# A state-space scan on one core: sums of h\*C in four 64x64 tiles of TensorE, and dt\*u\*B of every state by whole 128x128 products

## The chip, the cores and the metric

The kernel runs on one core of a Trainium2 chip. A core has TensorE (matrix products into PSUM, 8 banks of 512 fp32 per partition), VectorE, ScalarE and GpSimd (elementwise work), and SyncE, whose queue issues DMA transfers here. The engines run their own instruction streams and meet at semaphores. The metric is the device time of one execution in microseconds (us), lower is better, as a median of several runs.

## The reference

A decoder of two layers on 8 sequences of 128 tokens with 256 features, all in fp32. The change lies in the second layer's first part, a state-space (Mamba) block with 512 inner channels and 16 states per channel:

```
xz = einsum('bld,ed->ble', rmsnorm(x) * norm_w, in_proj_w);  x_inner, z = split(xz)
xc = silu(causal_conv4(x_inner) + conv_b)
x_ssm = einsum('bld,ed->ble', xc, x_proj_w)            # 16 B, 16 C, 1 dt per token
dt = softplus(x_ssm[..., -1:] * dt_w + dt_b);  A = -exp(A_log)
for each token t:                                       # per channel and state
    h = exp(dt_t * A) * h + (dt_t * u_t) * B_t          # u = xc
    y_t = sum over states (h * C_t) + D_param * u_t
out = einsum(y * silu(z), out_proj_w) + residual
```

Ahead of it lie two attentions and a mixture of experts, behind it a WKV recurrence and a ternary feed-forward part. The change does not touch those.

## The kernel before

Channels lie on partitions (4 channel tiles, `CT`, of 128), the 1024 tokens along the free axis. The scan loop has `SLOTS` = 64 slots, one for each channel tile and state. Slot s belongs to state `state(s)` and channel tile `channels(s)`: the first 32 slots take channel tiles 0 and 1 in turn through the 16 states, the last 32 take tiles 2 and 3. The hand-written streams do for each slot:

- ScalarE, `decay(s)` (L1694): dA = exp(dt \* A) into one of four buffers.
- TensorE, `dBu_in(s)` (L1523): makes dt\*u\*B in PSUM, in one of two pairs of banks (4, 5 and 6, 7). States 0, 4, 8, 12 are `DIRECT`: B's row is spread over the partitions by a bf16 product with a selector (L1529; B was split by GpSimd into three bf16 parts, `split`), and VectorE multiplies it by dt\*u in place (`dBu_of`, L1824). The other states are "turned": dt\*u was once transposed to tokens on partitions (`turn_dtu`, L1520; ScalarE's copy `turned_dtu`, L1682), ScalarE scales it by B per token (`scaled`, L1709, eight instructions of 128x256 for the two slots of a state), and eight transposes (L1536) turn it back.
- VectorE, `scan(s)` (L1834): one `tensor_tensor_scan` of 128x1024 gives h.
- GpSimd (L1911): hC = h \* C, where C's row was spread over the partitions by a DMA (SyncE, L1440).
- TensorE, `y_sum(s)` (L1548): adds hC to y in PSUM banks 0 to 3, by two products with the identity (L1557), one for each half of the tokens, 128 rows and 512 columns. For a channel tile's first state `skip_term` (L1546) adds D\*u in the same way.

TensorE's order in the loop is written out: at step s first `dBu_in(s + 1)`, which waits until scan s-1 has freed the banks, then `y_sum(s - 2)`. At the end two of the four channel tiles are projected out early (L1586 to L1590, rows at L1424), then come the last two y sums, and VectorE's gates (L1841). An fp32 product shows in the trace as two MATMUL records (two passes), a transpose as one.

Before the loop: GpSimd gathers the experts' rows (L1873), VectorE adds them up (`combine`) and takes the norm (L1332 to L1334). ScalarE writes the selector (`sel`, L1597), takes magnitudes of the last part's weights, makes the ternary weights (L1341 to L1344), and then the root that L1332 waits for. TensorE does the input projections (L1446), six of the eight tiles of z behind the rest of the prelude, B, C and dt rows (L1460), and dt's spread (L1467). VectorE and ScalarE make dt (`steps`, `exponentials`, L1677, `dt_and_dtu`, L1773 and L1775).

Two other places of the kernel, in the attentions and the expert part, use parts of the TensorE array: `values` (L676) writes two products of 64 output rows each to the partitions 0 to 63 and 64 to 127, between whole products of lines L658, L648, L667 and L686, and the bias products of L1472 have 32 rows each:

```python
for e in range(2):     # L675, in values(i)
    t = eng.matmul(ps[e * R:(e + 1) * R, 5, 0:2 * P], layer[name]["kvn"][:, b, :], prT[:, i % 2, :, e, :],
                   start=True, stop=True)
...
for b in range(NB):    # L1470
    rows = slice((b % 4) * E, (b % 4 + 1) * E)
    t = eng.matmul(ps[:, b, 0:D], weightT[rows, b // 4], bias_dn[rows],
                   start=True, stop=True)
```

Of the whole ones, `queries` (L648, with 96 rows) and `scores` (L658) are four products each in eight records, `turn_probs` (L667) is four transposes in four, and `output` (L686) two products in four.

## Time and profile before

| | us |
|---|---|
| median of 3 runs | 880.86 (879.38 to 882.98) |
| the profiled execution | 879.86 |
| its span | 877.7 |
| TensorE busy | 722.6 (82%) |
| VectorE busy | 695.3 (79%) |
| ScalarE busy | 550.1 (63%) |
| GpSimd busy | 515.2 (59%) |

The span is that of the instructions, and the rest of the profiled execution's time lies around it. Times in the rows are microseconds from the span's start, unless a row gives mean ns. PE is TensorE's products, PEld its weight loads, DVE VectorE, ACT ScalarE, POOL GpSimd, and L1834 is line 1834 of the kernel. The ends of TensorE's records are modelled and overlap the next record, so its pace is read from starts. The busy shares are means over stages with different limits. They do not say what a slot of the scan costs.

### The profile page before, as it was taken

The page shows a single profiled execution, that of the slowest core. Times are in us where ns is not written, and L with a number is a line of the kernel's source. Part 1 is how long each engine was busy: PE and PEld are TensorE (multiplying, and loading weights), DVE is VectorE, ACT ScalarE, POOL GpSimd, SP SyncE. Part 2 cuts the span into 40 slices and gives each one's busy share as a digit, 9 for nine tenths or more (in the row PEclk, how much of TensorE's full clock was granted, in tenths as well). Part 3 has the DMA queues.
Part 4 walks back from the last instruction along what each step waited for, and adds up shares of the span by engine and source line. Part 5 has one row for each costly group of instructions (what it writes and reads, how often), then busy time and mean ns, then how long its engine had stood idle before and what let it go on. Part 6 is the DMA issues. An engine that isn't in the chain of part 4 may idle for free. (4 is left out here: it accounts for less than half of the span.)

```text
span 877.7 us, 14518 instructions
## 1 busy us (share of the span) xinstructions
PE 722.6 (82%) x4318; PEld 530.6 (60%) x4321; DVE 695.3 (79%) x1515; ACT 550.1 (63%) x1383; POOL 515.2 (59%) x545
## 2 busy tenths in 40 slices
PE   5899999999999886299999149869899999961465
PEld 3588888888888774198897024345455555641333
DVE  6777788888898874877787456796999999769957
ACT  2545555555565553276676766688998788209286
POOL 2067777777777863255553572437999899624211
PEclk9999999999999999599999559979999999995679
DMA  8735000000000500058857330032322223010001
GB/s 318 240 145 240 1 1 1 8 1 7 8 1 7 206 7 13 19 165 214 237 164 124 90 102 19 3 119 70 99 97 96 87 92 110 0 49 0 0 13 36
DMA packets 30171, 70.52 MB, mean 80 GB/s; under 512 B 5456, under 2 KB 19472, under 8 KB 28176
## 3 DMA queue, kind: packets, MB, share of 16 engines
q1 hardware_dynamic: 25536, 57.15, 18.5%
q0 software_dynamic: 4560, 12.46, 6.6%
q8 instruction: 36, 0.59, 0.3%
q14 instruction: 39, 0.32, 0.1%
HBM read 59.17 MB, written 10.42 MB: 79 GB/s over the span
## 5 line engine op out<-in xcount | busy, mean ns | idle before, releaser
L1911 POOL TENSOR_TENSOR arena<-arena 128x1024 f32<-128x1024 f32 x63 | 148.5, 2387 | 38.6 <-DVE arena L1834 23.4
L1834 DVE TENSOR_TENSOR_SCAN arena<-arena,ps 128x1024 f32<-128x1024 f32 x64 | 143.9, 2277 | 15.1 <-PE ps L1536 8.0
L1557 PE MATMUL ps<-arena 128*128 128x512 f32 x256 | 120.1, 592 | 0.0
L648 PE MATMUL ps<-arena 128*128 128x128 f32 (+1 forms) x768 | 101.5, 283 | 0.9 <-PEq L376 0.9
L648 PEld LDWEIGHTS ps<-arena 128*128 128x128 f32 (+1 forms) x768 | 92.1, 194 | 13.7 <-issue 12.6
L853 ACT ACTIVATE arena<-arena 128x128 f32<-128x128 f32 x256 | 98.8, 390 | 1.2 <-DVE arena L777 1.1
L1089 POOL DMA_INDIRECT arena<-tokens,arena x63 | 60.7, 964 | 59.5 <-PE ps L1125 42.3
L861 ACT ACTIVATE arena<-ps 128x512 f32<-128x512 f32 x64 | 38.2, 597 | 86.6 <-PE ps L667 86.6
L1694 ACT ACTIVATE arena<-arena 128x1016 f32<-128x1016 f32 x64 | 72.2, 1135 | 18.2 <-DVE arena L1834 18.1
L1709 ACT ACTIVATE arena<-arena 128x256 f32<-128x256 f32 x192 | 81.3, 495 | 0.1
L908 POOL TENSOR_TENSOR arena<-arena 128x512 f32<-128x512 f32 x64 | 66.7, 1043 | 22.5 <-DVE arena L783 22.5
L898 POOL TENSOR_TENSOR arena<-arena 128x256 f32<-128x256 f32 x64 | 47.7, 745 | 45.3 <-DVE arena L763 45.3
L686 PE MATMUL ps<-arena 128*128 128x256 f32 x256 | 67.2, 386 | 5.3 <-DVE arena L788 5.3
L658 PEld LDWEIGHTS ps<-arena 128*128 128x128 f32 x512 | 67.3, 193 | 6.8 <-POOL arena L904 2.8
L658 PE MATMUL ps<-arena 128*128 128x128 f32 x512 | 68.6, 277 | 1.4 <-POOL arena L904 1.3
L1536 PEld LDWEIGHTS ps<-arena 128*128 128x128 f32 x384 | 45.1, 144 | 40.4 <-issue 25.6
L1137 PE MATMUL ps<-arena 128*128 128x128 f32 x504 | 67.6, 278 | 0.0
L1557 PEld LDWEIGHTS ps<-arena 128*128 128x128 f32 x256 | 45.2, 190 | 35.6 <-issue 33.3
L1137 PEld LDWEIGHTS ps<-arena 128*128 128x128 f32 x504 | 62.2, 194 | 0.2 <-ACT arena L1181 0.2
L1536 PE MATMUL ps<-arena 128*128 128x128 f32 x384 | 52.1, 281 | 12.1 <-ACT arena L1709 7.9
L760 DVE TENSOR_TENSOR arena<-ps,arena 128x512 f32<-128x512 f32 x64 | 43.4, 678 | 19.7 <-PE ps L648 19.0
L772 DVE TENSOR_TENSOR arena<-ps,arena 128x512 f32<-128x512 f32 x64 | 43.8, 684 | 16.3 <-PE ps L658 16.3
(330 smaller groups left out, 1610.8 us busy)
## 6 DMA issues: line engine op xcount, KB each, us to landing
arena<-c_rows SPq DMA_DIRECT2D x32, 512.0 KB, 3.6
arena<-in_E_gu SPq DMA_DIRECT2D x8, 1024.0 KB, 13.4
expert_out<-arena SPq DMA_DIRECT2D x63, 128.0 KB
arena<-in_E_dn SPq DMA_DIRECT2D x1, 4096.0 KB, 12.9
arena<-in_ctxT SPq DMA_DIRECT2D x2, 1024.0 KB, 5.1
arena<-in_A_o SPq DMA_DIRECT2D x1, 2048.0 KB, 15.5
arena<-in_X_o SPq DMA_DIRECT2D x1, 2048.0 KB, 21.9
arena<-in_F_w SPq DMA_DIRECT2D x4, 512.0 KB, 5.5
```

The costliest lines, as they stand in the source:

```text
L648: t = eng.matmul(ps[:, i % 2, j * P:(j + 1) * P], L["wq"][0:L["kc"], c, GH * g + j, :], src[0:L["kc"], c, b * P:(b + 1) * P], start=c == 0 ...
L658: t = eng.matmul(ps[:, 2 + i % 2, j * P:(j + 1) * P], q[:, i % NG, j, :], layer[name]["key"][:, j % 2, b * P:(b + 1) * P], start=True, sto ...
L686: t = eng.matmul(ps[:, BANK_O[name], 0:D], uT[:, i % 2, j, :], layer[name]["wvo"][:, GH // 2 * g + j, :], start=g == 0 and j == 0, stop=g ...
L853: t = eng.activation(pr[:, i % 3, j, :], sm[:, d, j, :], ACT.Exp, bias=negm[:, d, j:j + 1], scale=SCALE[slots[i][0]], accum_out=rsum[:, i ...
L908: eng.tensor_tensor(pr[:, i % 3], pr[:, i % 3], rinv[:, i % 3].unsqueeze(2).to_broadcast([P, GH, P]), ALU.mult).then_inc(pr_ready, 1)
L1137: t = eng.matmul(ps[:, 2 + d, k * I:(k + 1) * I], wcur[:, d, c, k * I:(k + 1) * I], xinT[:, d, c, :], start=c == 0, stop=c == DC - 1)
L1536: t = eng.transpose(psD[d][:, b // 4, at:at + P], sT[:, j % 2, b, k * P:(k + 1) * P], ident)
L1557: t = eng.matmul(ps[:, 2 * k + r, :], ident, half(hC[s % 4], r), start=False, stop=n == ST - 1)
L1694: eng.activation(dA[s % 4].rearrange(t8, b=NB)[:, :, 1:P], dts[:, c].rearrange(t8, b=NB)[:, :, 1:P], ACT.Exp, scale=negA[:, ST * c + n:ST ...
L1709: eng.activation(sT[:, j % 2, b, :], dtuT[:, b, 2 * cp:2 * cp + 2, :].rearrange("p c m -> p (c m)"), ACT.Copy, scale=B_tok[:, b, n:n + 1]) ...
L1834: eng.tensor_tensor_scan(hst[s % 4], dA[s % 4], psD[s % 2].rearrange("p k m -> p (k m)"), 0.0, ALU.mult, ALU.add).then_inc(h_ready, 1)
L1911: eng.tensor_tensor(hC[s % 4], hst[s % 4], Csb[i % 4], ALU.mult).then_inc(hC_ready, 1)
```

## The change

It rewrites how TensorE is used in the scan, and what feeds it.

1. dt\*u\*B for every state, direct ones too: `dBu(s)` does eight fp32 products of 128x128 by 128 columns, dt\*u with tokens on partitions as the stationary operand, and a diagonal of B's 128 tokens as the moving one. ScalarE writes these diagonals (`scaled(i)`, eight instructions of 128x128 per state, used for both slots), GpSimd the first two. The selector, the split into bf16 parts, the multiply on VectorE and the transposes back are gone.
2. y sums by pairs of slots: `y_pair` in two phases, one per slot's step. In a phase, slot a's partitions 0 to 63 and slot b's partitions 64 to 127 are added, each with both halves of the tokens, by four 64x64 products of 512 columns into four banks. The second phase swaps the roles. The second half of the tokens comes out with its 64-partition halves swapped. To match, z's second half is projected in swapped 64-column pieces (`gate_rows`), and `out_project` uses a weight with swapped rows, `w_out_sw`, a new load of 512 KB. The last two slots go through `y_last`.
3. Order: all six late z tiles, then the turned dt\*u, before the loop. All four `dt_and_dtu` come before scan 0. Both first gates come after scan 34. The residual's steps move from GpSimd to ScalarE, eight instructions of 128x256. x_proj's product has 33 columns instead of 97.

```diff
-        sel = view(51104, 2048, "p (e m) -> p e m", dt=bf16, e=E)
...
+        w_out_sw = view(51104, 1024, "p (k m) -> p k m", k=CT)
+        diagB = view(4096, 2 * NB * P, "p (d b m) -> p d b m", d=2, b=NB)
...
-        Z_BANK = (5, 6, 4, 5, 6, 2, 3, 0)
+        Z_BANK = (5, 6, 4, 5, 6, 2, 3, 7)
...
+            w = w_out if b < HB else w_out_sw
             for c in tiles:
-                t = eng.matmul(ps[:, 4 + b % 4, 0:D], yg[:, c, b * P:(b + 1) * P], w_out[:, c, :],
+                t = eng.matmul(ps[:, 4 + b % 4, 0:D], yg[:, c, b * P:(b + 1) * P], w[:, c, :],
...
+                load(eng, "w_out_sw", w_out_sw, a["M_out_swapped"])
...
-                            t = eng.matmul(ps[0:3 * E + 1, PROJ_BANK[k], :], w_bc[:, c, :], half(xc[:, c], k),
+                            t = eng.matmul(ps[0:E + 1, PROJ_BANK[k], :], w_bc[:, c, :], half(xc[:, c], k),
...
-                    project(CT + m, Z_BANK[n], k).then_inc(z_done, 1)
+                    if k == 0:
+                        t = project(CT + m, Z_BANK[n], k)
+                    else:
+                        for c in range(DC):
+                            for e in range(2):
+                                at = (CT + m) * P + e * R
+                                t = eng.matmul(ps[(1 - e) * R:(2 - e) * R, Z_BANK[n], :], w_in[:, c, at:at + R],
+                                               half(hT[:, c], k), start=c == 0, stop=c == DC - 1)
+                    t.then_inc(z_done, 1)
...
-                def dBu_in(s):
+                def dBu(s):
+                    i, c, d = state(s), channels(s), s % 2
                     if s >= 2:
                         eng.wait_ge(h_ready, s - 1)
-                    n, k, d = state(s) % ST, s % 2, s % 2
-                    if direct(s):
+                    if i < 2:
+                        eng.wait_ge(diagB_first, i + 1)
+                    else:
+                        eng.wait_ge(diagB_ready, i - 1)
+                    eng.wait_ge(dtuT_ready, c + 1)
+                    for b in range(NB):
+                        at = (b % HB) * P
+                        t = eng.matmul(psD[d][:, b // HB, at:at + P], dtuT[:, b, c, :], diagB[:, i % 2, b, :],
+                                       start=True, stop=True)
+                    t.then_inc(dBu_done, 1)
+
+                def y_rows(s, r, weights, src, start, stop):
+                    k = s % 2
+                    rows = slice(r * R, (r + 1) * R)
+                    for e in range(2):
+                        to = slice((r ^ e) * R, ((r ^ e) + 1) * R)
+                        t = eng.matmul(ps[to, 2 * k + e, :], weights[rows, rows], half(src[rows], e), start=start, stop=stop)
+                    return t
+
+                def y_pair(s, phase):
+                    eng.wait_ge(hC_ready, s + 2)
+                    if phase:
+                        eng.wait_ge(y_part, s // 2 + 1)
+                    elif s:
+                        eng.wait_ge(y_done, s)
+                    first, last = state(s) % ST == 0, state(s) % ST == ST - 1
+                    if first and not phase:
+                        if s:
+                            eng.wait_ge(y_gated, 2)
+                        else:
+                            eng.wait_ge(dtuT_ready, CT)
+                            eng.wait_ge(diag_in, KCONV + CT)
+                    mine = (s + phase, s + 1 - phase)
+                    if first:
                         for r in range(2):
-                            t = eng.matmul(psD[d][:, r, :], sel[0:3 * E, n, :], half(bc3[0:3 * E], r), start=True, stop=True)
-                        t.then_inc(B_done, 1)
-                        return
-                    j = turned_before(state(s))
-                    eng.wait_ge(sT_ready, NB * (j + 1))
-                    for b in range(NB):
-                        at = (b % 4) * P
-                        t = eng.transpose(psD[d][:, b // 4, at:at + P], sT[:, j % 2, b, k * P:(k + 1) * P], ident)
-                    t.then_inc(dBuT_done, 1)
-
-                def skip_term(s):
-                    c, k = channels(s), s % 2
-                    if c >= 2:
-                        eng.wait_ge(y_gated, k + 1)
+                            c = channels(mine[r])
+                            y_rows(mine[r], r, diagD[:, c], xc[:, c], True, False)
+                    for r in range(2):
+                        t = y_rows(mine[r], r, ident, hC[mine[r] % 4], False, last)
+                    if phase:
+                        t.then_inc(y_done, 2)
                     else:
-                        eng.wait_ge(dtuT_ready, 3 + k)
-                    for r in range(2):
-                        eng.matmul(ps[:, 2 * k + r, :], diagD[:, c], half(xc[:, c], r), start=True, stop=False)
-
-                def y_sum(s):
-                    k, n = s % 2, state(s) % ST
-                    if n == 0:
-                        skip_term(s)
+                        t.then_inc(y_part, 1)
+
+                def y_last(s):
+                    k = s % 2
                     if s == SLOTS - 1:
                         eng.wait_ge(hC_last, 1)
                     else:
                         eng.wait_ge(hC_ready, s + 1)
-                    for r in range(2):
-                        t = eng.matmul(ps[:, 2 * k + r, :], ident, half(hC[s % 4], r), start=False, stop=n == ST - 1)
+                    eng.wait_ge(y_done, s)
+                    eng.matmul(ps[:, 2 * k, :], ident, half(hC[s % 4], 0), start=False, stop=True)
+                    for e in range(2):
+                        t = eng.matmul(ps[(1 - e) * R:(2 - e) * R, 2 * k + 1, :], ident[:, e * R:(e + 1) * R],
+                                       half(hC[s % 4], 1), start=False, stop=True)
                     t.then_inc(y_done, 1)
 
-                eng.wait_ge(z_moved, 2)
-                eng.wait_ge(bc3_ready, 2)
-                eng.wait_ge(sel_ready, 1)
-                dBu_in(0)
+                for b in range(NB):
+                    t = eng.transpose(ps[:, 7, b * E:(b + 1) * E], bcf[0:E, b * P:(b + 1) * P], ident[0:E, 0:E])
+                t.then_inc(btok_done, 1)
+                for n in range(Z_FIRST, 2 * CT):
+                    if n == 2 * CT - 1:
+                        eng.wait_ge(btok_ready, 1)
+                    gate_rows(n)
+                eng.wait_ge(abs_ready, 2 * CT)
+                eng.wait_ge(zz_ready, 2 * CT)
+                turn_dtu(0)
+                eng.wait_ge(z_copied, 2)
+                turn_dtu(1)
                 eng.wait_ge(z_moved, Z_MOVED)
-                dBu_in(1)
-                eng.wait_ge(zz_ready, 2 * CT)
-                for b in range(NB):
-                    t = eng.transpose(ps[:, 1, b * E:(b + 1) * E], bcf[2 * E:3 * E, b * P:(b + 1) * P],
-                                      ident[2 * E:3 * E, 2 * E:3 * E])
-                t.then_inc(btok_done, 1)
-                for n in range(Z_FIRST + Z_MOVED, 2 * CT):
-                    gate_rows(n)
+                dBu(0)
+                turn_dtu(2)
+                eng.wait_ge(z_copied, Z_COPIED)
+                dBu(1)
+                turn_dtu(3)
                 for s in range(SLOTS + 2):
                     if 0 < s < SLOTS - 1:
-                        dBu_in(s + 1)
-                    if s == 0:
-                        eng.wait_ge(btok_ready, 1)
-                        eng.wait_ge(z_copied, Z_COPIED)
-                        turn_dtu(0)
-                        turn_dtu(1)
-                    if s == 2:
-                        turn_dtu(2)
-                        turn_dtu(3)
-                        eng.wait_ge(diag_in, KCONV + CT)
+                        dBu(s + 1)
                     if s == SLOTS:
-                        loaded(eng, "w_out")
+                        loaded(eng, "w_out", "w_out_sw")
                         eng.wait_ge(y_gated, 2)
                         eng.wait_ge(h_ready, SLOTS)
                         for b in range(4):
                             out_project(eng, b, (0, 1))
-                    if s >= 2:
-                        y_sum(s - 2)
+                    if 3 <= s < SLOTS + 1:
+                        pair = (s - 3) // 2 * 2
+                        y_pair(pair, (s - 3) % 2)
+                for s in range(SLOTS - 2, SLOTS):
+                    y_last(s)
 
...
-                eng.wait_ge(id3_ready, 1)
-                eng.activation(sel[0:3 * E], id3[0:3 * E].unsqueeze(2).to_broadcast([3 * E, E, P]), ACT.Copy).then_inc(sel_ready, 1)
...
+                eng.wait_ge(btok_done, 1)
+                eng.activation(B_tok, ps[:, 7, 0:NB * E].rearrange("p (b e) -> p b e", b=NB), ACT.Copy).then_inc(btok_ready, 1)
...
-                def scaled(i, first, end):
-                    n, cp, j = i % ST, i // ST, turned_before(i)
-                    if n in DIRECT:
-                        return
-                    if j == 0:
-                        eng.wait_ge(btok_ready, 1)
-                        eng.wait_ge(dtuT_ready, 2)
-                    if n == 1 and cp:
-                        eng.wait_ge(dtuT_ready, CT)
-                    if j >= 2 and first == 0:
-                        eng.wait_ge(dBuT_done, 2 * (j - 1))
-                    for b in range(first, end):
-                        eng.activation(sT[:, j % 2, b, :], dtuT[:, b, 2 * cp:2 * cp + 2, :].rearrange("p c m -> p (c m)"),
-                                       ACT.Copy, scale=B_tok[:, b, n:n + 1]).then_inc(sT_ready, 1)
-
-                for i in range(2 * ST):
-                    scaled(i, 0, NB // 2)
+                def scaled(i):
+                    n = i % ST
+                    eng.wait_ge(dBu_done, 2 * (i - 1))
+                    for b in range(NB):
+                        t = eng.activation(diagB[:, i % 2, b, :], ident, ACT.Copy, scale=B_tok[:, b, n:n + 1])
+                    t.then_inc(diagB_ready, 1)
+
+                def residual(b):
+                    eng.activation(x[:, b, :], x[:, b, :], ACT.Identity, bias=mean_rstd[:, b:b + 1], scale=rstd[:, b:b + 1])
+
+                gate_copy(Z_FIRST + Z_MOVED)
+                turned_dtu(0)
+                for n in range(Z_FIRST + Z_MOVED + 1, 2 * CT):
+                    gate_copy(n)
+                turned_dtu(1)
+                decay(0)
+                decay(1)
+                turned_dtu(2)
+                decay(2)
+                turned_dtu(3)
+                scaled(2)
+                decay(3)
+                for i in range(2, 2 * ST):
                     decay(2 * i)
+                    if i + 1 < 2 * ST:
+                        scaled(i + 1)
+                    decay(2 * i + 1)
                     if i == 2:
-                        turned_dtu(i)
-                    scaled(i, NB // 2, NB)
-                    decay(2 * i + 1)
-                    if i == 0:
-                        for n in range(Z_FIRST + Z_MOVED, 2 * CT):
-                            gate_copy(n)
-                        turned_dtu(0)
-                        turned_dtu(1)
-                    if i == 2:
-                        turned_dtu(i + 1)
-                    if i == ST // 2:
+                        eng.wait_ge(normS.h_ready, NB)
+                        eng.wait_ge(res_step, 5)
+                    if i - 2 < NB:
+                        residual(i - 2)
+                    if i == ST // 2 + 2:
...
-                def dBu_of(s):
-                    eng.wait_ge(B_done, direct_before(s) + 1)
-                    psB = psD[s % 2].rearrange("p k m -> p (k m)")
-                    eng.tensor_tensor(psB, dtu[:, channels(s)], psB, ALU.mult).then_inc(dBu_ready, 1)
...
-                dt_and_dtu(1)
+                for c in range(CT):
+                    dt_and_dtu(c)
                 eng.wait_ge(c_stored, 32)
-                eng.wait_ge(dtu_ready, 2)
                 for s in range(SLOTS):
-                    if direct(s):
-                        dBu_of(s)
                     scan(s)
-                    if s == 1:
-                        dt_and_dtu(2)
-                        dt_and_dtu(3)
-                    if s == 2 * ST - 1:
-                        eng.wait_ge(dtu_ready, CT)
-                    if s in (2 * ST + 1, 2 * ST + 2):
-                        gate(s - 2 * ST - 1)
+                    if s == 2 * ST + 2:
+                        gate(0)
+                        gate(1)
...
+                eng.wait_ge(btok_ready, 1)
+                for i in range(2):
+                    eng.tensor_tensor(diagB[:, i], ident.unsqueeze(1).to_broadcast([P, NB, P]),
+                                      B_tok[:, :, i:i + 1].to_broadcast([P, NB, P]), ALU.mult).then_inc(diagB_first, 1)
...
-                    if s % 6 == 5 and s // 6 < NB:
-                        b = s // 6
-                        eng.tensor_scalar(x[:, b, :], x[:, b, :], rstd[:, b:b + 1], mean_rstd[:, b:b + 1], ALU.mult,
-                                          ALU.subtract)
...
+    mo = chunked(g["L1_attn_out_proj_w"].T)
+    put("M_out", mo)
+    put("M_out_swapped", np.concatenate([mo[R:], mo[:R]]))
```

## Rows read from the trace of the kernel before

**Rows 1.** Groups of instructions by line and shape, window 597 to 757 us.

```profile
L1911 POOL TENSOR_TENSOR arena<-arena 128x1024 f32<-128x1024 f32 x58 | 135.9, 2374 | 17.6 <-DVE arena L1834 17.6
L1834 DVE TENSOR_TENSOR_SCAN arena<-arena,ps 128x1024 f32<-128x1024 f32 x59 | 132.6, 2277 | 14.6 <-PE ps L1536 7.7 <-issue 4.2 <-ACT arena L1694 1.4
...
L1694 ACT ACTIVATE arena<-arena 128x1016 f32<-128x1016 f32 x58 | 65.6, 1135 | 18.2 <-DVE arena L1834 18.1
L1536 PE MATMUL ps<-arena 128*128 128x128 f32 x354 | 46.8, 275 | 6.4 <-DVE arena L1834 4.1 <-ACT arena L1709 2.3
```

**Rows 2.** Timeline of TensorE, 640 to 645 us: start, length, engine, line, operation.

```profile
641.62 1.88 PE L1557 MATMUL ps<-arena 128*128 128x512 f32 x4
643.34 1.04 PE L1536 MATMUL ps<-arena 128*128 128x128 f32 x8
```

**Rows 3.** Timeline of VectorE in the same loop; in brackets idle time before and releaser.

```profile
632.93 1.21 DVE L1824 TENSOR_TENSOR ps<-arena,ps 128x1024 f32<-128x1024 f32 x1
634.22 4.69 DVE L1834 TENSOR_TENSOR_SCAN arena<-arena,ps 128x1024 f32<-128x1024 f32 x2
...
641.88 2.29 DVE L1834 TENSOR_TENSOR_SCAN arena<-arena,ps 128x1024 f32<-128x1024 f32 x1 [0.38 <-PE ps L1536]
644.47 2.29 DVE L1834 TENSOR_TENSOR_SCAN arena<-arena,ps 128x1024 f32<-128x1024 f32 x1 [0.31 <-PE ps L1536]
```

**Rows 4.** Timeline of TensorE in an attention slot, whole and tiled products.

```profile
206.45 1.05 PE L658 MATMUL ps<-arena 128*128 128x128 f32 x8
207.43 0.65 PE L676 MATMUL ps<-arena 128*64 128x256 f32 x4
208.01 1.16 PE L648 MATMUL ps<-arena 96*128 96x128 f32 x8
209.01 0.60 PE L667 MATMUL ps<-arena 128*128 128x128 f32 x4
209.45 1.03 PE L686 MATMUL ps<-arena 128*128 128x256 f32 x4
210.31 1.05 PE L658 MATMUL ps<-arena 128*128 128x128 f32 x8
```

**Rows 5.** Line L1472 by itself: durations min/median/max in ns, first and last start.

```profile
L1472 PE MATMUL ps<-arena x16: 629/629/788, 487.9 to 489.3; 32*128 32x256 f32 x16
```

**Rows 6.** Timeline of all engines, 565 to 606 us, ahead of the loop and its start.

```profile
567.82 3.90 ACT L1677 ACTIVATE arena<-arena 128x1024 f32<-128x1024 f32 x4
...
568.91 1.23 DVE L1773 SCALAR_TENSOR_TENSOR arena<-arena 128x1024 f32<-128x1024 f32 x1 [1.27 <-ACT arena L1677]
...
571.74 1.28 ACT L1694 ACT_TABLE_LOAD   x1
...
575.11 1.55 ACT L1652 ACTIVATE arena<-ps 128x512 f32<-128x512 f32 x3
575.55 2.29 DVE L1834 TENSOR_TENSOR_SCAN arena<-arena,ps 128x1024 f32<-128x1024 f32 x1
...
578.69 1.02 ACT L1682 ACTIVATE arena<-ps 128x1024 f32<-128x1024 f32 x1 [2.03 <-PE ps L1520]
...
603.73 2.29 DVE L1834 TENSOR_TENSOR_SCAN arena<-arena,ps 128x1024 f32<-128x1024 f32 x1 [0.31 <-PE ps L1536]
```

**Rows 7.** Timeline of all engines, 480 to 548 us, the prelude.

```profile
488.17 3.62 ACT L1597 ACTIVATE arena<-arena 96x4096 bf16<-96x4096 f32 x1 [3.90 <-DVE arena L1777]
...
496.65 1.26 ACT L1607 ACTIVATE arena<-arena 128x128 f32<-128x128 f32 x4
...
515.77 0.18 DVE L1332 RECIPROCAL arena<-arena 128x4 f32<-128x4 f32 x1 [3.92 <-ACT arena L1325]
```

**Rows 8.** Timeline of all engines, 750 to 785 us, the loop's end.

```profile
757.93 2.29 DVE L1834 TENSOR_TENSOR_SCAN arena<-arena,ps 128x1024 f32<-128x1024 f32 x1 [0.30 <-PE ps L1536]
...
761.12 3.62 PE L1424 MATMUL ps<-arena 128*128 128x256 f32 x16
...
768.20 1.22 DVE L1841 TENSOR_TENSOR arena<-ps,arena 128x1024 f32<-128x1024 f32 x1 [0.43 <-PE ps L1557]
```

64 lines of the change are left out of this document (13 added, 51 removed).

## The prediction

> **What bounds the kernel now.** The chain that ended last reaches back over the last layer only, so I went by stage instead. First the scans' line by itself: 64 scans, from the first to the last start, take 575.55 to 757.93 us [rows 6, 8]. Then the groups by line in the steady part of that loop, then the waits, then the order of time inside single slots.
>
> In the steady part the reader sees no engine full on average [rows 1]: a scan costs VectorE 2.28 us, an h\*C product costs GpSimd 2.37 us, a decay costs ScalarE 1.14 us. VectorE's idle time before scans is named after TensorE's transposes (L1536) more than after anything else. Inside one slot [rows 2] it is plain why. The four passes of the y sum start at 641.62, the next slot's eight transposes 1.72 later at 643.34, nothing idle between: 4 x 0.43 + 8 x 0.11 = 2.6 us of TensorE per slot, and VectorE's scans come 2.59 us apart with a 0.31 us wait for TensorE in front of each [rows 3]. So a slot of a "turned" state is bound by TensorE. A slot of a direct state is bound by VectorE: its extra product of 1.21 us makes it 3.5 us (the product of 632.93 and the scan behind it in [rows 3]). Twelve states of one kind and four of the other, with TensorE catching up behind the direct ones, give (757.93 - 603.73) / 57 = 2.705 us per slot between slot 6 and slot 63 [rows 6, 8].
>
> **The change, part by part.** *The plain slot.* VectorE loses the 1.21 us product of the direct states, GpSimd loses eight residual steps. Neither sets the end unless TensorE becomes faster than they are. TensorE decides.
>
> It gets, per slot, eight whole fp32 products of 128 columns in place of eight transposes. A transpose is one record, a product two (L667, four records for four transposes, against L658, eight for four products). The records start 0.11 us apart in both (209.01 to 209.45 in [rows 4]). So dt\*u\*B costs 16 x 0.11 = 1.76 us per slot (before: 0.88, and nearly nothing in direct states).
>
> It gets, per slot, one phase of the y sum: four 64x64 tiles of 512 columns, two passes each. If the four run at once, that is 2 x 0.43 = 0.86 us in place of 1.72. What speaks for it: L676 puts two products in the two column halves, each with its own moving operand from the same partitions, and its four records take 0.58 us from first start to the next line's start, where L686's four records of the same 256 columns take 0.86 [rows 4]. L1472 runs products of 32 rows each, and starts all sixteen records of 256 columns within 1.4 us [rows 5]: one after the other, at L686's 0.215, fifteen steps would need 3.2 at least, so three or four go at once. Rows and columns both halved, as here, no row shows. The four tiles write four different banks, which is what L1472 does too.
>
> But every phase stands between two groups of whole-array products, and the rows put a price on that. L658's eight records should take 0.88 us and the next line starts 0.98 later, because that line is tiled. L676's pairs should take 2 x 0.215 = 0.43 and take 0.58. L648's eight records behind it should take 0.88 and take 1.00 [rows 4]. In, inside and out: 0.10 + 0.15 + 0.12 = 0.37 us for a round trip (the 0.11 rounded up; with 0.1115 it is 0.35). I read it as the array running dry at each change of tile shape, with the weight load, otherwise hidden, laid bare. The Trainium skill says the same in kind ("TensorEngine Tiling (Array Packing)", Tiling Modes: changing the mode, not just the tile, drains TensorE) and gives no price. By the same page of the Trainium skill, Overview, which counts only an up to fourfold speedup for four tiles, the slot would be 2.62 (an estimate with the rows' 1.76 and 0.86). By the rows it is 2.99.
>
> Slot after: 1.76 + 0.86 + 0.37 = 2.99, say 3.0 us, all on TensorE, above the scan's 2.28 and GpSimd's 2.37, and above ScalarE's share: per pair of slots two decays and eight diagonals, 2 x 1.14 + 8 x 0.315 ([rows 1, 7], L1607 is the same operation) = 4.8 of 6.0 us. Chains hold too: scan s ends about 1.8 us before TensorE wants to start dBu(s+2), and hC waits for the end of a pair's second phase, 4.8 us of GpSimd work in 6.0. 57 slots: 57 x 3.0 = 171.0 against 154.2 now, **+16.8**. From slot 0 to slot 63 the loop has two skip-term phases per channel pair. For the first pair they are counted below; the second adds 2 x 0.86. The two gates (1.22 each [rows 8]) are now both after slot 34 and wait for the end of pair 30's second phase; scan 35 stands behind them. Followed slot by slot that costs 2.9 including the skip terms: **+2.9**.
>
> *The first slots.* On the old clock [rows 6]: softplus's logarithms run 567.82 to 571.7, dtu is ready at 568.91 + 2 x 1.23 = 571.4, then every 2.46 us. ScalarE now does, ahead of the first decay, a gate copy (0.52), the turned copy of channel tile 0 (transposes until 572.6, copy 1.02, until 573.7), two gate copies (574.8), turned copy 1 (575.5 to 576.5), the table load 1.28, decay 1.13. Scan 0 starts at 578.9 instead of 575.55. But now all four dtu come before it, and turned copies 2 and 3 only delay decay 3 (580.0 + 1.0 + 1.1 + 1.0 + 2.5 + 1.1 = 586.8). Scans 0 to 4 start at 578.9, 581.2, 583.5, 586.9, 589.2. TensorE has the skip phases (4 x 0.43 + 0.2) between dBu(4), dBu(5), dBu(6): scan 5 at 591.9, scan 6 at 596.0, against 603.73 now. **-7.7**, give or take 2. TensorE's six gate tiles all come before the loop now; they end near 571, when dtu is ready, so I cost them at nothing. Without that cover the last one would cost 1.7. GpSimd's two first diagonals (2.4 each) take the place of the splits and are done some 10 us before use.
>
> *The prelude.* ScalarE's selector copy L1597 (3.62 us, starting at 488.17) goes. What stands behind it in that queue is without a gap up to the square root whose result VectorE's L1332 waits 3.92 us for at 515.77 [rows 7]. So that wait nearly goes: -3.6 (3.62 removed, and the reciprocal cannot come earlier than 3.92). Later the expert rows gathered by GpSimd pace VectorE, which gives some back for the second half; TensorE's queue, which is behind the first half, keeps most. **-3.3**, bounds -3.9 and 0. x_proj with 33 output columns becomes a tile of its own shape: some passages more, up to 0.37 each, **+0.5**. The new 512 KB load of the swapped weights is queued on SP beside the gathers; it is needed 270 us later. Nothing, at worst 2 us of slower gathers.
>
> *The tail.* From the last scan's start to the end of the last gate it is 757.93 to 769.42 now, with TensorE on out_project 3.4 us and two y sums [rows 8]. After, behind out_project come the last pair's second phase (0.86), and two y_last of 4 passes each, part whole, part tiled, with three more changes of shape, while the 0.9 us by which TensorE trails now is gone: **+1.1**.
>
> Sum: -3.3 + 0.5 - 7.7 + 16.8 + 2.9 + 1.1 = **+10.3 us**. The profiled execution took 879.86 (span 877.7, 2.2 around it), so 890.2; the median of the runs shown, 880.86, stands 1.0 above it. I say **890.5**. Something like 0.5% (4.4 us) is what a measurement here can tell from no change.
>
> **The rivals.** *A: the passage in and out is hidden in the loop* (say it is the price of L676's short operands and not of the change of shape; 512 columns stream longer than any weight load). Then the slot is 2.62, the loop 57 x 0.37 = 21 us shorter: 869. Against it: the time lost is at both ends, in front of whole products of 128 columns exactly like the ones here, and the gap inside (0.05) is a weight load that has nothing earlier to hide under. For it: no row of a 64x64 group between whole ones. The point from which it decides: break-even is a slot of 3.0 - 10.3 / 57 = 2.82 us, a round trip of 0.2. Chance 0.20.
>
> *B: the four tiles do not all run at once.* With two at a time a phase is 4 x 0.43 = 1.72, the slot 3.85: 57 x 0.86 = 49 more, 939. If a product's two passes must end before the next tile's first, it is five passes: 2.15 a phase, about 964. The Trainium skill ("TensorE: Matmul & The Clock Gate", Part 3) has matmuls in strict order of the program, by which this could happen. Against both: L676's two tiles lose nothing to it [rows 4], row tiles do run at once, more than two of them [rows 5]. Chance 0.08.
>
> *C: no change.* Slot at 2.85 to 2.9 because part of the passage hides under waits, or prelude and start give 5 us more than I have. 877 to 884. Chance 0.10.
>
> *The forecast,* 884 to 900: 0.62.
>
> **How the numbers follow.** Rival A and the forecast hold 0.82; the range goes from A's middle down a little, 867, to 900, and takes in C. Left out are B and the ends of the others. Faster by over 0.5% (below 876.5): A, 0.20. Same: C and the forecast's lower edge, 0.11. Slower: 0.69. The likeliest case alone has 884 to 898.
>
> **What would show it.** Right: plain slots of scans 2.95 to 3.05 us apart with a wait for dBu in front of each, TensorE near 100% busy there; dBu's sixteen records and the four tiles' eight records with 0.48 between the first starts of the two passes; scan 0 about as late as now and scan 6 clearly earlier; the selector copy's place gone and L1332's wait with it. Wrong: slots of 2.6 (A), or 3.8 and more (B), or a wait for decays or diagonals (ScalarE), which would mean that I undercount its 4.8 us per pair.

## The result, and the profile after

The changed kernel takes 893.65 us (median of 4 executions, 892.46 to 895.14), the kernel before 880.29 beside it: a ratio of 1.0148, interval 1.012 to 1.0175. That is 13.4 us more. The profiled execution took 895.14 us with a span of 892.8, against 879.86 and 877.7; so the traces differ by 15.1 us of span. The forecast was 890.5, in a range of 867 to 900. The profiled execution of the changed kernel is the slowest of its four, and that of the kernel before lies 0.4 us under its median. So 1.7 us of the difference of the traces are chance.

Groups by line and shape of the kernel after, 597 to 770 us (answers to [rows 1]; busy time, mean ns of one, then the idle time before them and what ended it):

```profile
L1898 POOL TENSOR_TENSOR arena<-arena 128x1024 f32<-128x1024 f32 x58 | 135.9, 2362 | 42.3 <-PE ps L1535 39.9 <-DVE arena L1838 2.4
L1838 DVE TENSOR_TENSOR_SCAN arena<-arena,ps 128x1024 f32<-128x1024 f32 x57 | 130.1, 2285 | 40.4 <-PE ps L1526 37.4 <-ACT arena L1709 2.9
L1526 PE MATMUL ps<-arena 128*128 128x128 f32 x909 | 116.8, 281 | 0.2 <-DVE arena L1838 0.2
...
L1716 ACT ACTIVATE arena<-arena 128x128 f32<-128x128 f32 x216 | 66.1, 388 | 34.7 <-PE ps L1526 34.7
L1535 PE MATMUL ps<-arena 64*64 64x512 f32 x472 | 63.8, 614 | 0.6 <-POOL arena L1898 0.6
```

(The window is 13 us longer than that of [rows 1], as the loop is.) VectorE's idle time has grown from 14.6 to 40.4 us, GpSimd's from 17.6 to 42.3, and ScalarE has 34.7: nearly all of it names TensorE, whose own two lines wait for 0.8 us in 173. TensorE is the bound, and alone. The same in order of time, one slot near the end of the loop and the next one's start:

```profile
765.60 2.05 PE L1526 MATMUL ps<-arena 128*128 128x128 f32 x16
...
767.58 1.09 PE L1535 MATMUL ps<-arena 64*64 64x512 f32 x8
767.74 2.29 DVE L1838 TENSOR_TENSOR_SCAN arena<-arena,ps 128x1024 f32<-128x1024 f32 x1 [0.71 <-PE ps L1526]
768.60 2.05 PE L1526 MATMUL ps<-arena 128*128 128x128 f32 x16
```

From dBu's first start to the next dBu's first start it is 768.60 - 765.60 = 3.00 us: 1.98 for dBu's sixteen records, 1.02 for the four tiles ([rows 2] had 1.72 + 0.88). Line L1535 by itself, first in that stretch and then up to 768.0 alone, shows that the eight records of four tiles lie in two groups half a microsecond apart, not in a row of eight (minimum, median and maximum of one in ns, first and last start):

```profile
L1535 PE MATMUL ps<-arena x8: 589/614/640, 767.6 to 768.1; 64*64 64x512 f32 x8
L1535 PE MATMUL ps<-arena x4: 640/640/640, 767.6 to 767.6; 64*64 64x512 f32 x4
```

Four records start within 0.02 us and the other four 0.48 us behind them. So all four tiles run at once, each pass for all of them. By stage, in the two profiled executions, where the 15.1 us come from:

| stretch | before | after | difference | forecast |
|---|---|---|---|---|
| up to the first logarithm | 567.82 | 567.56 | -0.3 | -2.8 |
| first logarithm to scan 0 | 7.73 | 12.83 | +5.1 | +3.35 |
| scan 0 to scan 6 | 28.18 | 16.71 | -11.5 | -11.1 |
| scan 6 to scan 63 | 154.20 | 173.64 | +19.4 | +19.7 |
| scan 63 to the end of the last gate | 11.49 | 12.97 | +1.5 | +1.1 |
| from there to the end | 108.3 | 109.1 | +0.8 | 0 |

Most of what the forecast misses lies ahead of scan 0. Timeline of the kernel before there, from the addition of the down projection's biases (L1786), which is the anchor for the times "after the bias additions" in the experiments:

```profile
489.14 2.48 DVE L1786 TENSOR_TENSOR arena<-arena,ps 128x512 f32<-128x512 f32 x4 [0.84 <-PE ps L1472]
...
560.72 0.79 DVE L1768 TENSOR_SCALAR arena<-arena 128x512 int32<-128x512 int32 x1
...
562.26 1.23 DVE L1768 TENSOR_SCALAR arena<-arena 128x512 int32<-128x512 int32 x1
...
566.53 1.28 ACT L1677 ACT_TABLE_LOAD   x1
```

And the same stretch of the kernel after:

```profile
489.78 2.48 DVE L1802 TENSOR_TENSOR arena<-arena,ps 128x512 f32<-128x512 f32 x4 [0.97 <-PE ps L1461]
...
512.52 1.28 ACT L1324 ACT_TABLE_LOAD   x1 [1.47 <-DVE arena L1318]
...
514.05 0.18 DVE L1331 RECIPROCAL arena<-arena 128x4 f32<-128x4 f32 x1 [1.61 <-ACT arena L1324]
...
558.97 3.96 POOL L1890 TENSOR_TENSOR arena<-arena 128x1024 f32<-128x1024 f32 x2 [20.59 <-ACT arena L1688]
559.26 1.90 DVE L1786 TENSOR_SCALAR arena<-arena 128x512 int32<-128x512 int32 x1
...
561.91 1.30 DVE L1786 TENSOR_SCALAR arena<-arena 128x512 int32<-128x512 int32 x1
...
566.26 1.28 ACT L1692 ACT_TABLE_LOAD   x1
567.56 3.90 ACT L1692 ACTIVATE arena<-arena 128x1024 f32<-128x1024 f32 x4
...
571.28 1.94 PE L1512 MATMUL ps<-arena 128*128 128x128 f32 x8 [2.25 <-DVE arena L1793]
...
574.82 1.97 PE L1512 MATMUL ps<-arena 128*128 128x128 f32 x8 [1.60 <-ACT arena L1665]
...
580.39 6.79 DVE L1838 TENSOR_TENSOR_SCAN arena<-arena,ps 128x1024 f32<-128x1024 f32 x3 [2.08 <-ACT arena L1709]
```

Three things stand here that the forecast did not have. The run is already 0.64 us late at the bias additions (489.78 against 489.14), ahead of the changed block. That is chance: the kernel of experiments 3 and 12, one and the same, gets there at 493.61 and 489.87 us. The reciprocal's wait goes from 3.92 [rows 7] to 1.61 and not to nothing: the square root's table load (1.28 us) and the root itself stand behind the variances in both kernels, so only the rest of the wait could go. And GpSimd's first two diagonals lie beside VectorE's absolute values, which take 1.90 and 1.30 us where they take 0.43 undisturbed. In the kernel before, GpSimd's splits lay beside them too, and they took 0.79 and 1.23. Behind that, the first two groups of transposes take 1.94 and 1.97 us; the granted clock tells why (windows of the kernel after: busy time of each engine, PEclk, DMA):

```profile
571.00:573.00 2.00, 1.72 (x8) 1.57 (x8) 1.97 (x3) 0.94 (x2) 0.00 (x0) 0.56 0.83 272
573.00:575.00 2.00, 0.40 (x3) 0.18 (x2) 1.97 (x3) 1.75 (x3) 0.00 (x0) 0.50 1.02 371
```

Behind 2.25 us of idle time the clock is at 0.50, its lower level (1.2 GHz), and eight transposes cost twice their 1.0 us. The trace of the kernel before had the same to show. Its first two groups of transposes of dt\*u (line L1520) stand behind 2.50 us of idle time, and the clock is at 0.50 there (a row of TensorE's timeline, then a window):

```profile
576.76 3.60 PE L1520 MATMUL ps<-arena 128*128 128x128 f32 x16 [2.50 <-issue]
```

```profile
577.00:580.00 3.00, 3.00 (x16) 2.96 (x14) 2.90 (x3) 1.02 (x1) 0.86 (x1) 0.50 0.94 384
```

One profile of each kernel is not the whole story either. Experiments 2, 5 and 9 below have the changed kernel's code up to the logarithms, and in their profiles the table load for the logarithms stands 75.3 to 75.8 us after the bias additions. In the changed kernel's own profile it is 76.5, in that of the kernel before 77.4. So the prelude gains 0.9 us in this profile and 1.6 to 2.1 in the three others.

### The profile page after: what moved, and what is told of

Read it like the earlier page. It is cut to its first block and busy times, and to the rows that moved or that the text cites. A ratio compares the mean times of both kernels' runs of the same rounds, so it can differ in the third digit from the quotient of the medians.

```text
span 892.8 us, 16401 instructions
## 1 busy us (share of the span) xinstructions
PE 752.0 (84%) x5213; PEld 570.4 (64%) x5213; DVE 677.3 (76%) x1497; ACT 543.0 (61%) x1439; POOL 499.1 (56%) x528
## 5 line engine op out<-in xcount | busy, mean ns | idle before, releaser
L1838 DVE TENSOR_TENSOR_SCAN arena<-arena,ps 128x1024 f32<-128x1024 f32 x64 | 145.9, 2285 | 44.8 <-PE ps L1526 38.1
L1526 PEld LDWEIGHTS ps<-arena 128*128 128x128 f32 x1024 | 119.9, 193 | 49.1 <-issue 45.4
L1526 PE MATMUL ps<-arena 128*128 128x128 f32 x1024 | 131.8, 282 | 0.5 <-DVE arena L1838 0.4
L852 ACT ACTIVATE arena<-arena 128x128 f32<-128x128 f32 x256 | 98.8, 389 | 1.2 <-DVE arena L776 1.1
L1716 ACT ACTIVATE arena<-arena 128x128 f32<-128x128 f32 x240 | 73.4, 388 | 34.7 <-PE ps L1526 34.7
L657 PEld LDWEIGHTS ps<-arena 128*128 128x128 f32 x512 | 67.5, 194 | 6.6 <-POOL arena L903 2.6
L1535 PE MATMUL ps<-arena 64*64 64x512 f32 x528 | 71.0, 613 | 0.8 <-POOL arena L1898 0.6
L1709 ACT ACTIVATE arena<-arena 128x1016 f32<-128x1016 f32 x64 | 70.0, 1128 | 0.0
L657 PE MATMUL ps<-arena 128*128 128x128 f32 x512 | 68.9, 278 | 1.3 <-POOL arena L903 1.3
L1136 PE MATMUL ps<-arena 128*128 128x128 f32 x504 | 68.7, 281 | 0.0
L1136 PEld LDWEIGHTS ps<-arena 128*128 128x128 f32 x504 | 63.5, 197 | 0.1
L685 PEld LDWEIGHTS ps<-arena 128*128 128x128 f32 x256 | 43.8, 191 | 9.4 <-issue 5.9
## 6 DMA issues: line engine op xcount, KB each, us to landing
arena<-in_E_dn SPq DMA_DIRECT2D x1, 4096.0 KB, 13.4
```

The lines of the kernel that those rows point to most:

```text
L657: t = eng.matmul(ps[:, 2 + i % 2, j * P:(j + 1) * P], q[:, i % NG, j, :], layer[name]["key"][:, j % 2, b * P:(b + 1) * P], start=True, sto ...
L685: t = eng.matmul(ps[:, BANK_O[name], 0:D], uT[:, i % 2, j, :], layer[name]["wvo"][:, GH // 2 * g + j, :], start=g == 0 and j == 0, stop=g ...
L852: t = eng.activation(pr[:, i % 3, j, :], sm[:, d, j, :], ACT.Exp, bias=negm[:, d, j:j + 1], scale=SCALE[slots[i][0]], accum_out=rsum[:, i ...
L1136: t = eng.matmul(ps[:, 2 + d, k * I:(k + 1) * I], wcur[:, d, c, k * I:(k + 1) * I], xinT[:, d, c, :], start=c == 0, stop=c == DC - 1)
L1526: t = eng.matmul(psD[d][:, b // HB, at:at + P], dtuT[:, b, c, :], diagB[:, i % 2, b, :], start=True, stop=True)
L1535: t = eng.matmul(ps[to, 2 * k + e, :], weights[rows, rows], half(src[rows], e), start=start, stop=stop)
```

## The experiments

The first question was the terms of the slot: would they come out alone as they do together? The second was where the prelude's 3.3 us went. The ratios in brackets are to the kernel before, timed beside each group of runs: 880.18 for the first four, 880.03 for the next four, 879.36 for the last four.

**1. dt\*u\*B by whole products, y sums whole as before.**

```diff
-    for e in range(2):
-        to = slice((r ^ e) * R, ((r ^ e) + 1) * R)
-        t = eng.matmul(ps[to, 2 * k + e, :], weights[rows, rows], half(src[rows], e), start=start, stop=stop)
+    for e in range(2):
+        t = eng.matmul(ps[:, 2 * k + e, :], weights, half(src, e), start=start, stop=stop)
```

> Undoes one part of the change: the y sums are whole 128x128 products of 512 columns again (and z's second half and the output weight unswapped), dt*u*B stays as in the change. No change of tile shape is left in the loop. Forecast's theory (four tiles at once, 0.86 us a phase, plus 0.35 us for the passage in and out): a plain slot is 16 x 0.1115 + 4 x 0.43 = 3.50 us, 0.50 above the change's 3.00; 57 slots give +28, the time is about 920. Rival (the passage costs nothing, and the change's slot of 3.00 has another reason, such as a wait): the slot grows by the whole 0.86 to 3.86, about 941. If the tiles bring nothing (they run two at a time): the slot stays at 3.0.

927.21 us (2 executions; ratio 1.0521, 1.0477 to 1.0566). TensorE's timeline:

```profile
661.36 1.95 PE L1519 MATMUL ps<-arena 128*128 128x128 f32 x16
663.14 1.88 PE L1526 MATMUL ps<-arena 128*128 128x512 f32 x4
664.86 1.95 PE L1519 MATMUL ps<-arena 128*128 128x128 f32 x16
```

Slot 3.50 us: 1.78 for sixteen records and 1.72 for four, with no loss where one kind of whole product follows the other. So the 1.98 that dBu takes in the changed kernel has 0.20 of passage in it, and the four tiles' 1.02 has 0.16 over the 0.86 of two passes. The loop from scan 6 to 63 is 204.1 us, 30.5 more than in the changed kernel where 28 were expected; scans 0 to 6 take 2.7 more and the way from scan 63 to the last gate 1.4 more, which the expectation of 920 did not count.

**2. Two passages per slot instead of one:** each phase of y is issued in two halves of 256 columns, one in the middle of dBu's products and one behind them; the arithmetic is the same.

```diff
-    dBu(s + 1)
-    y_pair(pair, (s - 3) % 2)
+    dBu(s + 1, 0)
+    y_pair(pair, (s - 3) % 2, 0)
+    dBu(s + 1, 1)
+    y_pair(pair, (s - 3) % 2, 1)
```

> Doubles one suspected cost: each phase of the y sum is cut into its first and its last 256 columns, one part between the fourth and fifth of the eight dt*u*B products, the other behind the eighth. The same columns are streamed, but each slot goes into the tiled shape and out of it twice. Forecast's theory: 0.35 us more per plain slot, 3.35 us, some 57 x 0.35 = 20 more, about 914. Rival (the passage is hidden or is a matter of waits once per slot): no more than 0.03 us per slot for the four records more, about 895.

917.34 us (2 executions; ratio 1.0409, 1.0369 to 1.045). TensorE, then VectorE's last wait in that stretch:

```profile
663.38 1.16 PE L1526 MATMUL ps<-arena 128*128 128x128 f32 x8
664.47 0.66 PE L1541 MATMUL ps<-arena 64*64 64x256 f32 x8
665.06 1.16 PE L1526 MATMUL ps<-arena 128*128 128x128 f32 x8
```

```profile
667.99 2.29 DVE L1852 TENSOR_TENSOR_SCAN arena<-arena,ps 128x1024 f32<-128x1024 f32 x1 [1.08 <-PE ps L1526]
```

Slot 3.36: the second round trip costs 0.36 us, with the same columns streamed. This is the price of the passage measured by itself, and rival A, in which it is hidden, falls.

**3. Both kinds of sums in 64x64 tiles.** The four tiles of a product write the four quarters of the state tile; B's diagonal is kept for half as many columns (two identities of 64 side by side are folded into one), and dt\*u, C and the x_proj rows are written in an order of columns in which the scan can still read one run.

```diff
-    t = eng.matmul(psD[d][:, b // HB, at:at + P], dtuT[:, b, c, :], diagB[:, i % 2, b, :], ...)
+    for r in range(2):
+        rows = slice(r * R, (r + 1) * R)
+        for e in range(2):
+            t = eng.matmul(psD[d][e * R:(e + 1) * R, r, b * R:(b + 1) * R],
+                           dtuT[rows, b, c, e * R:(e + 1) * R], diagB[rows, i % 2, b], ...)
```

> Takes the changes of shape away without going back: dt*u*B is made in 64x64 tiles too. A diagonal has nothing off its diagonal, so 64 tokens of contraction and 64 columns do for each half: four tiles of 64 columns at a time, row half 0 always in one bank and row half 1 always in the other (the tokens are paired over the two banks for that), diagonals half as wide on ScalarE. Same output. Forecast's theory: no passages, 0.86 us for y, and 16 groups of four tiles in 0.06 us each (weight load of 64 columns), 0.96; TensorE needs 1.8 to 1.9 us per slot, and GpSimd's 2.36 or VectorE's 2.29 becomes the bound: a slot of 2.35 to 2.4, 57 x 0.63 = 36 less than the change, 855 to 860. Rival (small tiled products are bound by the rate at which TensorE takes instructions, as far as 0.025 us a record): 64 x 0.025 + 0.86 = 2.5, about 866. If tiles of 64 columns do not run together: above 3 us, slower than the change.

858.15 us (4 executions, 856.61 to 860.69; ratio 0.9732, 0.9699 to 0.9765). TensorE's timeline, three rows of VectorE's, and the groups by line from scan 6 to scan 63 (594.35 to 737.68 us):

```profile
683.86 1.14 PE L1535 MATMUL ps<-arena 64*64 64x64 f32 x64
684.79 1.07 PE L1544 MATMUL ps<-arena 64*64 64x512 f32 x8
685.65 0.83 PE L1535 MATMUL ps<-arena 64*64 64x64 f32 x41
...
699.61 0.33 PE L1535 MATMUL ps<-arena 64*64 64x64 f32 x4 [1.94 <-issue]
```

```profile
636.91 2.29 DVE L1850 TENSOR_TENSOR_SCAN arena<-arena,ps 128x1024 f32<-128x1024 f32 x1 [3.01 <-ACT arena L1718]
639.85 26.24 DVE L1850 TENSOR_TENSOR_SCAN arena<-arena,ps 128x1024 f32<-128x1024 f32 x12 [0.66 <-ACT arena L1718]
...
700.05 8.86 DVE L1850 TENSOR_TENSOR_SCAN arena<-arena,ps 128x1024 f32<-128x1024 f32 x4 [1.40 <-ACT arena L1718]
```

```profile
L1911 POOL TENSOR_TENSOR arena<-arena 128x1024 f32<-128x1024 f32 x58 | 135.3, 2378 | 10.5 <-PE ps L1544 7.5 <-DVE arena L1850 3.0
L1850 DVE TENSOR_TENSOR_SCAN arena<-arena,ps 128x1024 f32<-128x1024 f32 x58 | 128.4, 2269 | 14.0 <-ACT arena L1718 6.9 <-PE ps L1535 4.8 <-issue 2.0
L1535 PE MATMUL ps<-arena 64*64 64x64 f32 x3648 | 74.5, 224 | 19.3 <-issue 16.1 <-DVE arena L1850 2.7
```

Where nothing holds TensorE up, dBu takes 0.93 us (684.79 - 683.86) in place of 1.98, and y 0.86 (685.65 - 684.79) in place of 1.02, without passages: 1.79 us for a slot, as expected. That is also the price of four tiles at once, 0.86, read from a row and not from a difference. The expectation's rival, 0.025 us for a record, falls: 64 records in 0.93 us are 0.015 each.

Now TensorE's own work is no longer the bound. Twelve scans run with nothing between, (26.24 - 2.29) / 11 = 2.18 us apart. But the loop from scan 6 to 63 is 143.3 us, 2.51 a slot, and not 124. The fullest engine is GpSimd, with 135.3 us of h\*C products, and the rest is in stalls. At the one of 3.01 us ScalarE had two table loads and the silu of the gates between its decays. Others begin in TensorE: 17 times in this loop, 16.1 us in all, it stands still in the middle of dBu's records while the profile names no releaser. Ahead of 699.61 it does so for 1.94 us, with four of the 64 records left, and the scan of 700.05, which needs them, has waited 1.40 us. The row names a decay, but the one that this scan reads had ended at 695.53, and the last of dBu's records starts at 699.73. Ten scans start like that, within 0.13 us of the end of a dBu that had stalled, and 7.5 of VectorE's 14.0 us of idle time lie ahead of them. The changed kernel's loop has no such stall. These stalls come at regular distances, 110 to 119 of dBu's records or about a multiple of that. The kernel has four times as many of these records, and the queue that the profile's page calls "instruction" moves 68 packets (44 in the changed kernel). That TensorE waits for its instructions there is a guess from these figures, and no run tests it.

**4. The kernel before with only y in tiles** (pairs of slots, swapped weights for the second half of out_project; transposes, direct states, selectors stay). To make room for the swapped weight the selector holds only the four states in use, so its copy ahead of the loop takes 0.4 us instead of 3.6.

```diff
-    if s >= 2:
-        y_sum(s - 2)
+    if 3 <= s < SLOTS + 1:
+        y_pair((s - 3) // 2 * 2, (s - 3) % 2)
```

> The other half of the change alone: the kernel before with the y sums in pairs of 64x64 tiles, z and the output weight swapped; dt*u*B by the direct product in states 0, 4, 8, 12 and by transposes in the others, as before (the selector holds only the four states used, 0.4 us instead of 3.6 in the prelude, to make room for the swapped weight). Forecast's theory: TensorE needs 0.88 + 0.86 + 0.35 = 2.09 us in a turned state, so VectorE bounds: 12 slots of 2.2 and 4 of 3.43 give 2.51 on average against 2.705 before; ScalarE's 5.66 us per pair of turned slots (2.83 a slot) may hold some of them. 57 x 0.1 to 0.2 = 6 to 11 us less than before: 868 to 875. Rival (the tiled y sum is what costs the change its time, the whole products do not): slower than before, 885 or more.

872.17 us (4 executions; ratio 0.9892, 0.9861 to 0.9924). TensorE's timeline:

```profile
639.87 1.09 PE L1548 MATMUL ps<-arena 128*128 128x128 f32 x8
640.89 1.09 PE L1556 MATMUL ps<-arena 64*64 64x512 f32 x8
641.91 1.09 PE L1548 MATMUL ps<-arena 128*128 128x128 f32 x8
```

1.02 + 1.02 = 2.04 us for a turned slot in place of 2.60, below the scan's 2.18. By the rows of the kernel before, eight transposes are 0.87, so a round trip costs 2.04 - 0.87 - 0.86 = 0.31 us here. The 8.0 us are not y's alone: the shorter selector copy brings scan 0 3.4 us nearer to the bias additions (83.05 us after them instead of 86.41). By one profile of each, the tiles are worth 8.5 us between scans 0 and 63, less 1.5 from there to the last gate, 7.0 in all, passages included. The changed kernel loses that, and more, to the products that take the place of transposes and direct states: scans 6 to 63 take 173.6 us in it and 148.0 here.

**5. Five extra products ahead of the first transposes,** to keep TensorE busy in the 2.25 us.

```diff
+    for n in range(5):
+        eng.matmul(ps[:, 0, :], ident, half(zs[:, 0], 0), start=True, stop=True)
     turn_dtu(0)
```

> The changed kernel with five extra products of 128x512 on TensorE between its last tiled gate tile and its first transposes of dt*u (they write a bank that is free and that the transposes then overwrite; nothing of the computation changes). There TensorE idles 2.25 us, and the granted clock then is 0.54 and 0.50 over 571 to 577 us. Theory (the idle stretch costs the clock, and the slow transposes make the turned copies, the table load and the first decay late): the idle time falls under 0.3 us, the granted clock stays at 1.00, the two first groups of eight transposes take 1.0 to 1.1 us each instead of 1.94 and 1.97, and the first scan starts 1.5 to 1.9 us earlier against the addition of the down projection's biases (90.6 us after it now); the whole kernel 891 to 892.5. Rival (the clock falls for another reason, or the first scan waits for something else): the transposes stay at 1.9 us or become short with the first scan where it was, 893.6.

893.67 us (2 executions; ratio 1.0164, 1.0126 to 1.0203). TensorE's timeline:

```profile
568.78 4.56 PE L1586 MATMUL ps<-arena 128*128 128x512 f32 x10
...
573.18 1.04 PE L1512 MATMUL ps<-arena 128*128 128x128 f32 x8
```

Five fp32 products are ten records of 0.43 us, so the filler was 4.4 us long, twice what I meant, and held back the transposes it was to help. They run in 1.04 us at a granted clock of 1.00. The first scan comes 89.8 us after the bias additions (90.6 in the changed kernel's profile). In experiments 1 and 2, without a filler, it is 88.7 and 88.6, so the filler gained nothing. That the products kept the clock up agrees with the theory, but experiments 1, 2 and 7 have the first group fast (1.06 us) behind 2.25 to 2.40 us of idle time without them.

**6. The first diagonals later.**

```diff
     eng.wait_ge(btok_ready, 1)
+    eng.wait_ge(abs_ready, 2 * CT)
     for i in range(2):
         eng.tensor_tensor(diagB[:, i], ...)
```

> The changed kernel with one more wait on GpSimd: its two first products identity times B (3.96 us) begin only once VectorE is through with the absolute values of both halves, instead of beside them. Theory (the two engines slow each other, and the logarithms wait for VectorE): the absolute values of the second half take 0.43 us each instead of 1.90, 1.30, 0.43, 0.43; the logarithms start 2.2 to 2.4 us earlier (76.5 us after the bias additions now, 74.2 then); TensorE's idle time ahead of the first transposes falls under 0.5 us, so that these run at a granted clock of 1.00 in 1.04 us without any filler; the first scan starts 3.5 to 4 us earlier (90.6 now, 87 then); the whole kernel about 890. Rival (the logarithms wait for TensorE's x_proj products or for ScalarE): the logarithms move by under 0.5 us, the first scan by under 0.7, 893.5.

889.65 us (2 executions, 887.08 and 892.21; ratio 1.0118, 1.0068 to 1.0169). Timeline of all engines:

```profile
560.80 3.79 POOL L1891 TENSOR_TENSOR arena<-arena 128x1024 f32<-128x1024 f32 x2 [23.99 <-DVE arena L1786]
...
563.71 1.96 DVE L1791 SCALAR_TENSOR_TENSOR arena<-arena 128x1024 f32<-128x1024 f32 x1 [1.27 <-ACT arena L1692]
...
567.08 1.06 PE L1512 MATMUL ps<-arena 128*128 128x128 f32 x8 [0.64 <-DVE arena L1793]
```

All four absolute values take 0.43 us. The logarithms' table load starts 72.9 us after the bias additions (76.5 in the changed kernel's profile, 75.3 to 75.8 in experiments 2, 5 and 9, which leave this part alone), so 2.4 to 3.6 earlier. The collision has moved in part: the first product behind the logarithms takes 1.96 us instead of 1.23. TensorE's idle time is 0.64 us, its transposes take 1.06 and 1.09, and scan 0 starts at 86.0 instead of 90.6 (88.6 and 88.7 in experiments 1 and 2). The time of the whole kernel does not show it: the two executions are 5 us apart, and the interval overlaps that of the changed kernel.

**7. The square root's table loaded ahead of the variances.**

```diff
+    eng.activation(roots[:, 0, 0:1], ident[:, 0:1], ACT.Sqrt)
     eng.wait_ge(roots_in, k + 1)
     eng.activation(roots[:, 1, some], roots[:, 1, some], ACT.Sqrt)
```

> The changed kernel with one extra square root of a column of the identity on ScalarE ahead of its wait for the first variances, so that the table load (1.28 us) no longer stands between the variances and the reciprocal. Theory (the second half of the rows, which ends with GpSimd's gathers, decides when the steps begin, and the first half has slack): the first reciprocal comes 1.3 us earlier (24.3 us after the bias additions now, 23.0 then), the second half's variances move by under 0.3 us (43.7 now), and so do the logarithms and the first scan; the kernel 893 to 894. Rival (the first half decides): everything up to the first scan moves by 1.3 us, 892.3.

894.08 us (2 executions; ratio 1.0169, 1.0131 to 1.0206). The reciprocal comes 22.9 us after the bias additions instead of 24.3; the second half's variances stay (44.0 against 43.7), and the logarithms' load at 75.4 is where experiments 2 and 5 have it (75.3 and 75.4) without this edit. Scan 0 comes at 88.7 instead of 90.6, which looks like the rival, but experiments 1 and 2 have 88.7 and 88.6 without the edit, and the time of the kernel does not fall. The first half has slack; GpSimd's gathers pace the second half, and that decides. TensorE's timeline has something more:

```profile
571.36 1.06 PE L1513 MATMUL ps<-arena 128*128 128x128 f32 x8 [2.25 <-DVE arena L1794]
...
574.02 1.97 PE L1513 MATMUL ps<-arena 128*128 128x128 f32 x8 [1.60 <-ACT arena L1666]
```

The same 2.25 us of idle time, but here the clock falls one group later, as it does in experiments 1 and 2.

**8. Experiment 3 with the edits of 6 and 7.**

> The kernel with both kinds of sums in 64x64 tiles (the one that ran at 858.15) with the late first diagonals and the early square root table together. The diagonals there are half as wide (2.26 us of GpSimd) and cost the absolute values only 0.6 us; the last gate tile ends 0.55 us before the first transposes. Theory: the logarithms start 0.6 us earlier, then TensorE's gate tiles are what the transposes wait for; the first scan starts 0.4 to 0.6 us earlier (87.2 us after the bias additions there), the loop stays as it is at 2.46 us for a slot, set by GpSimd's 2.33 us for a product h*C and VectorE's 2.29 for a scan; 857 to 858. Rival (more of the prelude hangs on the two waits): the first scan 1.5 to 2 us earlier, 856.

855.64 us (4 executions, 853.4 to 860.77; ratio 0.9723, 0.9691 to 0.9755). Scan 0 at 85.5 us instead of 87.2, nearer to the rival's 1.5 to 2 us than to the theory's 0.5: the logarithms moved by 1.7 us, and the gate tiles were not in the way. A microsecond of it is lost again by scan 6, and the median lies at the rival's 856 too.

**9. Experiment 5 with two products instead of five.**

> The changed kernel with two extra products of 128x512 between its last gate tile and its first transposes, in place of the five of the run before, which took 4.56 us and were themselves in the way of the transposes. Two take about 1.8 us of the 2.25 us of idle time. Theory: TensorE idles under 0.6 us there, the granted clock stays at 1.00, both first groups of transposes take 1.0 to 1.1 us, and the first scan starts 87.9 to 88.9 us after the bias additions (90.6 in the changed kernel's profile, 89.8 with five); the kernel 892. Rival (the clock falls in the idle time behind the first transposes instead, 1.6 us): the second group takes 1.9 us again and the first scan starts at 88.7 to 89.5.

894.17 us (2 executions; ratio 1.0171, 1.0145 to 1.0198). TensorE's timeline:

```profile
570.90 1.09 PE L1512 MATMUL ps<-arena 128*128 128x128 f32 x8 [0.25 <-DVE arena L1795]
...
573.60 1.97 PE L1512 MATMUL ps<-arena 128*128 128x128 f32 x8 [1.60 <-ACT arena L1667]
```

The rival. The first group is fast, the clock falls behind it (a mean of 1.00 from 571 to 573 us, of 0.66 from 573 to 575, where TensorE is idle at first), and scan 0 starts at 88.95. Experiments 3, 5 and 6 have the same 1.60 us and keep 1.00; what tips it between them no run here shows.

**10. Experiment 8 with six of the 64 h\*C products on VectorE.**

```diff
     scan(s)
+    if s in (11, 19, 27, 43, 51, 59):
+        eng.tensor_tensor(hC[s % 4], hst[s % 4], Csb[i % 4], ALU.mult).then_inc(hC_vector, 1)
```

> The tiled-dBu kernel with the late diagonals and the early table, and with the h*C product of six of the 64 slots (11, 19, 27, 43, 51, 59) on VectorE in place of GpSimd. Theory (the loop there, 142.7 us for 57 slots, is paced by GpSimd's 57 x 2.33 = 133 us, and VectorE's scans alone would need 57 x 2.19 = 125): GpSimd's share falls by 6 x 2.3 = 14 us, VectorE's rises by 6 x 1.25 = 7.5 us, and the loop gets 2 to 6 us shorter; 851 to 854. Rival (beside GpSimd's own product VectorE's takes 2.5 us or more, or the two hold each other up): the loop stays within 1.5 us or gets longer, 855 to 860.

862.5 us (4 executions, 858.08 to 864.88; ratio 0.9794, 0.9766 to 0.9822). VectorE's products by themselves (minimum, median and maximum in ns):

```profile
L1872 DVE TENSOR_TENSOR arena<-arena x6: 1783/2682/3122, 607.5 to 730.1; 128x1024 f32<-128x1024 f32 x6
```

The rival: a median of 2.68 us for a product, and the loop from scan 6 to 63 grows from 142.7 to 147.0 us. GpSimd's busy time in it falls from 133.0 to 119.9 us and VectorE's rises from 128.1 to 142.6, so the bound has moved from one to the other. All six products end 1.08 to 1.09 us behind the end of the GpSimd product that had begun before them.

**11 and 12. Experiments 8 and 3 again, side by side.**

> The same kernel as e8, timed again beside the next one on the same chip, to tell whether late diagonals and the early table table are worth anything there. Theory (first scan 1.7 us earlier in its profile, one microsecond of it kept at slot 6): 1 to 2.5 us below the kernel without them. Rival: within 1 us.

> The kernel with both kinds of sums in 64x64 tiles and nothing else, timed again for the comparison with the run before: 857 to 859.

855.4 us (5 executions; ratio 0.9736, 0.9713 to 0.9758) against 857.49 (ratio 0.9756, 0.9736 to 0.9777; five executions of 856.5 to 859.73, and one of 1208.64 us that stands apart and is left out of the median). Both pairs of medians, this and the one of 3 and 8, differ the same way, by 2.1 and 2.5 us, and scan 0 comes 1.65 us earlier here as well (84.9 against 86.5). But the intervals overlap, so that the time of the kernel falls by it is likely and not shown.

## Why the prediction was right, and where its terms were off

**The slot, 2.99 forecast, 3.00 measured.** All three terms held: 1.78 for the whole products (experiment 1), 0.86 for four tiles at once (experiment 3), 0.36 for the round trip (experiment 2, by itself). The direction is no luck: the loop's +19.7 rests on these three. The parts stood in [rows 4] already, in another layer's small tiles of 256 columns. The rule of the Trainium skill ("TensorEngine Tiling (Array Packing)", Tiling Modes) that a change of mode drains the array agrees with these runs: 0.36 us for a round trip (experiment 2), 0.31 beside transposes (experiment 4). Rival A, a hidden passage, falls with it. Rival B's strict order of passes is not seen: the first passes of all four tiles start together, then the second ones.

**The loop.** +19.4 against +19.7 with gates and skip terms.

**The first slots.** From scan 0 to 6, -11.5 against -11.1. But the way from the first logarithm to scan 0 was mis-sized by 1.75 us: the forecast had "transposes until 572.6, copy 1.02", from transposes of 1 us. It let the gate tiles "end near 571, when dtu is ready", so it saw no idle time of TensorE; they ended at 569.0, 2.25 us earlier than the transposes could start. The transposes took 1.9 us twice in place of 1.04, and that makes the 1.75. Half of it is chance: in experiments 1, 2 and 7, with the same idle time or more, only the second group was slow. The sign "scan 0 about as late as now" did not come true (4.8 us later), "scan 6 clearly earlier" did (6.6).

**The prelude, -3.3 + 0.5 forecast, -0.3 measured.** This is the term furthest off. Of the 2.5 us between them 0.64 lie ahead of the changed block, and about one more is this profile's own, as the other profiles of the same code show. The step that failed is "-3.6 (3.62 removed, and the reciprocal cannot come earlier than 3.92)" as a gain of the whole. The reciprocal came 2.4 us earlier against the bias additions, since 1.61 us of the wait were the table load and the root behind the variances, and not the selector's; and of these not all counts, as the second half hangs on the gathers (experiment 7): its variances came 1.15 us earlier. Then "GpSimd's two first diagonals take the place of the splits and are done some 10 us before use" priced them by when they are needed and not by what they lie beside: absolute values of 1.90 and 1.30 us for 0.79 and 1.23, 1.2 us more, and 2.4 to 3.6 us at the logarithms when they are moved (experiment 6). The +0.5 for x_proj's passages was too much: from the products ahead of its second half (550.89 and 549.32 us) to dt's spread behind it (558.71 and 557.25) it is 7.82 us before and 7.93 after. The bound of 0 that I gave the prelude's gain held.

**The tail,** +1.5 against +1.1; and 0.8 us behind it, in code that the change doesn't touch, which I can't assign.

The sum was 10.3 us; the profiled executions differ by 15.1 and the medians by 13.4. Of the 4.8 that are missing in the profiles, 2.5 are the prelude's, 1.75 the clock's, 1.2 the tail's and what follows it, and the scans give 0.7 back. In the medians only 3.1 are missing, since the profiled execution of the changed kernel is 1.5 us above its median and that of the kernel before 0.4 below.

**The better version.** The changed kernel bought room for TensorE in y (7.0 us, experiment 4) and spent it, and more, on dBu's sixteen whole-array records. With those in 64x64 tiles too, a slot needs 1.79 us of TensorE and no passages, and the kernel takes 858.15, with the later diagonals and the earlier table 855.4 to 855.6: 2.6 to 2.8% under the kernel before.

## What to carry to other kernels

Put products of one tile shape next to each other: here a round trip between whole and quarter tiles costs 0.31 to 0.36 us, as much as three whole records of 128 columns. A diagonal or block-diagonal operand has the array multiply by zeros that tiles can leave out; here the same work takes 0.93 us instead of 1.78. And a stage that is removed from one engine's queue gives back only what the next waiter does not have from elsewhere: list the second-latest arrival (a table load, a gather, an operation of GpSimd beside VectorE's) before taking the whole length as gain. And compare stages against an anchor just ahead of the change, in more than one profile: here the same code reaches that anchor up to 3.7 us apart, and its way to scan 0 varies by 2.

## What the runs showed of the hardware that was not expected

- An fp32 product in tiles runs by passes over all tiles: four tiles, eight records, two groups of starts 0.5 us apart.
- VectorE beside a GpSimd product: an operation of 0.43 us took 1.90 (experiment 6 removes it), one of 1.23 took 1.96, and h\*C on VectorE 1.78 to 3.12 (experiment 10). They end at a fixed distance behind the GpSimd product that had begun before them: the absolute values of 1.90 and 1.30 us 0.28 us behind it, the product of 1.96 in experiment 6 1.08, as in experiment 10. So in these rows VectorE is held until GpSimd's product is done.
- The granted clock went to 0.50 behind 2.50 us of idle time in the kernel before and 2.25 in the changed kernel; behind 2.25 to 2.40 and then 1.60 us in experiments 1, 2 and 7; behind 0.25 and then 1.60 us in 9. It stayed at 1.00 through 0 to 0.64 and then 1.60 us in 3, 5, 6, 8, 10, 11 and 12. The same code with the same idle times (the changed kernel and experiment 2) lost it at different moments.
- 64 records of 64x64 tiles with 64 columns take 0.93 us up to the next line's start: 0.06 us for a group of four, against 0.11 for a whole record of 128 columns.
- With so many small records TensorE's stream has stalls of up to 2.0 us that name no releaser, 16.1 us in the middle of dBu's records between scans 6 and 63 of experiment 3, where the changed kernel has none. Their cause is open.
